# An expert layer's weights one block further ahead, written from another queue and spread in fewer, longer runs

## What is computed

```
def _moe(tokens, router_w, w1, b1, w2, b2):
    logits = tokens.astype(jnp.float32) @ router_w.astype(jnp.float32).T
    probs = jax.nn.softmax(logits, axis=-1)
    rw, re = jax.lax.top_k(probs, TOP_K)
    rw = rw / jnp.maximum(rw.sum(-1, keepdims=True), 1e-12)
    combine = jnp.zeros((N, E), tokens.dtype).at[jnp.arange(N)[:, None], re].set(rw)
    for e in range(E):
        h = jax.nn.gelu(tokens @ w1[e] + b1[e], approximate=False)
        y = h @ w2[e] + b2[e]
        out = out + combine[:, e:e + 1] * y
```

## Time and profile before

| | |
|---|---|
| median of 3 runs | 337.88 us (335.43 to 340.08) |
| the profiled execution | 335.06 us, of which the span of its engines is 333.2 us |
| mean granted clock of TensorE | 0.931 of full speed |
| PE busy | 287.0 us (86%) |
| DVE busy | 220.3 us (66%) |
| ACT busy | 153.3 us (46%) |
| POOL busy | 130.9 us (39%) |
| DMA, all queues | 23.53 MB, mean 71 GB/s |

### The profile page before, as it was taken

One profiled execution on the slowest core, in us unless ns is written; L12 is line 12 of the kernel. 1 busy time (PEld: TensorE's weight loads), 2 busy tenths in 40 slices (PEclk: granted clock), 3 DMA queues, 4 the chain that ended last, 5 costly groups with the idle time before them and its releaser, 6 DMA issues.

```text
span 333.2 us, 9456 instructions
## 1 busy us (share of the span) xinstructions
PE 287.0 (86%) x3821; PEld 184.6 (55%) x3821; DVE 220.3 (66%) x690; ACT 153.3 (46%) x290; POOL 130.9 (39%) x147
## 2 busy tenths in 40 slices
PE   0358799897989888988968999998989999999994
PEld 0348678786656655765645655664434444444551
DVE  5974456775688769667678599756244555557773
ACT  1693621004475465455643445468884454542000
POOL 7326505825995861500013189986008300000000
PEclk9996995555899999999999999999999999999999
DMA  6234000003797596687570000000000001000111
GB/s 229 69 69 94 5 2 2 0 3 85 177 228 165 135 240 165 154 208 188 143 181 2 2 2 1 2 3 3 0 0 2 20 16 33 31 27 8 34 48 48
DMA packets 16903, 23.53 MB, mean 71 GB/s; under 512 B 8052, under 2 KB 12700, under 8 KB 16860
## 3 DMA queue, kind: packets, MB, share of 16 engines
q1 hardware_dynamic: 16860, 22.94, 27.0%
HBM read 20.57 MB, written 2.36 MB: 69 GB/s over the span
## 4 chain that ended last, share of the span: by engine, by line
PE 53%; DVE 14%; DMA 12%; ACT 6%; issue 6%; POOL 5%; SPq 3%; DVEq 0%; POOLq 0%; ACTq 0%
PE pair L1756 8%; PE pair L1741 8%; DMA hid<-c_dram 7%; PE pair L1722 7%; PE pair L1612 5%; PE pair L1390 3%; DMA c_dram<-cT 3%; POOL ln_rstd L585 3%; DVE scaled L840 2%; PE pair L1400 2%; PE pair L1536 2%; PE pair L1563 2%; PE pair L1768 1%; DVE stats L739 1%; DMA xs_ffn<-c_dram 1%
## 5 line engine op out<-in xcount | busy, mean ns | idle before, releaser
L1101 DVE SCALAR_TENSOR_TENSOR hid<-pair,neg_shift,ln_x 128x512 f32<-128x512 f32 x64 | 45.1, 746 | 30.3 <-PE pair L1741 30.3
L1227 ACT ACTIVATE pair<-pair,cols 128x512 f32<-128x512 f32 x64 | 39.5, 656 | 31.0 <-PE pair L1536 30.8
L585 POOL TENSOR_TENSOR ln_rstd<-ln_var,neg_half 128x8 f32<-128x8 f32 x16 | 26.4, 1656 | 50.8 <-DVE ln_var L862 50.8
L1536 PE MATMUL pair<-xs,w1f 64*64 64x256 f32 x512 | 36.6, 402 | 4.2 <-DVE scaled L840 4.1
L1722 PE MATMUL pair<-xs_ffn,f1f 64*64 64x512 f32 x256 | 33.7, 599 | 1.6 <-ACT hid L1299 1.0
L1563 PE MATMUL pair<-scaled,w 64*64 64x256 f32 x512 | 35.0, 378 | 0.0
L1756 PE MATMUL pair<-hid,fo 64*64 64x256 f32 x512 | 34.1, 380 | 0.6 <-DVE hid L1101 0.6
L1612 PE MATMUL pair<-xp,vconv 64*64 64x256 f32 x512 | 32.4, 400 | 0.0
L1756 PEld LDWEIGHTS pair<-hid,fo 64*64 64x64 f32 x512 | 18.6, 133 | 19.9 <-issue 10.9
L840 DVE TENSOR_TENSOR scaled<-pair,hid 128x1024 f32<-128x1024 f32 x16 | 19.5, 1221 | 12.9 <-DMA hid<-c_dram 9.9
L1536 PEld LDWEIGHTS pair<-xs,w1f 64*64 64x64 f32 x512 | 18.2, 138 | 13.6 <-DVE scaled L840 6.0
(11 more groups left out here) (225 smaller groups left out, 559.6 us busy)
## 6 DMA issues: line engine op xcount, KB each, us to landing
xs_ffn<-c_dram SPq DMA_DIRECT2D x32, 256.0 KB, 6.0
hid<-c_dram SPq DMA_DIRECT2D x32, 256.0 KB, 5.4
out_dram<-x SPq DMA_DIRECT2D x8, 256.0 KB, 2.1
x<-in_x_dram SPq DMA_DIRECT2D x3, 512.0 KB, 6.2
x<-in_x_dram SPq DMA_DIRECT2D x2, 256.0 KB, 3.0
w1f<-in_L_ffn_w_dram SPq DMA_DIRECT2D x2, 128.0 KB
w<-in_L_ffn_w_dram SPq DMA_DIRECT2D x2, 128.0 KB
f1f<-in_L_ffn_W_dram SPq DMA_DIRECT2D x2, 128.0 KB
```

Of the source, the lines that this page charges most:

```text
L585: g.tensor_tensor(ln_rstd[:, st, b % 2, :], ln_var[:, st, b % 2, :], neg_half[:, 0:T2], ALU.pow).then_inc(ln_rstd_ready[st], 1)
L1101: v.scalar_tensor_tensor(out=hid2[:, n % 2, u, :].rearrange("p (j n) -> p j n", j=2), in0=h, scalar=neg_shift2[:, k, u:u + 1], in1=w, op0= ...
L1227: s.activation(h, h, ACT.Gelu, bias=cols[:, e:e + 1]).then_inc(hidden_gelu, 1)
L1536: last = t.matmul(pair[N % 2][halves(th), i, 2 * P * u:2 * P * (u + 1)], w1f[halves(i), C * e:C * (e + 1)], xs[halves(i), b % 3, 2 * P * t ...
```

## The change

- The spread is four transfers of 512 KB in 8 KB runs for a block in place of eight of 256 KB in 4 KB runs; the scales of groups 0 and 1 wait for the first two of them, those of groups 2 and 3 for the others.
- The write of cT to DRAM is issued by ACT, right behind its copy, in two halves of 32 rows; SP only waits until both have landed. cw and cT are widened to two halves of 64, the second half of each zero, and the transpose to 128 x 128, so that the halves start at partitions 0 and 64; the bias matmuls thereby work on pieces of 64 rows.
- In round b, DVE routes block b + 2 to the end (before: block b + 2 up to step 14, and the two last steps of block b + 1): steps 1 to 9 behind the scale of group 1, steps 10 to 14 ahead of that of group 3, and 15 and 16 behind it. PE and ACT follow in the order below.
- The scaled tile has three buffers in place of two.
- A gelu on a small tile is put ahead in the start-up, where it loads ACT's table.
- In the start-up the transposes of weights for blocks 0 and 1 stand further ahead, and the two first groups of block 0 in another place among the matmuls of the gates.

```diff
-        b2m = sb("b2m", [T2 * E, T2, C])
+        b2m = sb("b2m", [P, T, C])
...
-        scaled = sb("scaled", [P, 2, 2, 2, 2 * P])
+        scaled = sb("scaled", [P, 3, 2, 2, 2 * P])
...
-        cw = sb("cw", [P, T2 * E])
-        cT = sb("cT", [T2 * E, 2, P])
+        cw = sb("cw", [P, 2, C])
+        cT = sb("cT", [P, 2, P])
...
             for b in range(NB):
-                sp.wait_ge(c_copied, b + 1)
-                sp.dma_start(c_dram.ap()[b].rearrange("h e (r n) -> (h e r) n", r=T), cT[:, b % 2, :]).then_inc(c_written, 16)
-                sp.wait_ge(c_written, 16 * (b + 1))
-                for k in range(KP):
-                    wait(sp, hidden_scaled, KP * (b - 2) + k + 1)
+                sp.wait_ge(c_written[b % 2], 32 * (b // 2 + 1))
+                for k in range(KP // 2):
+                    wait(sp, hidden_scaled, KP * (b - 2) + 2 * k + 2)
                     wait(sp, c_spread[k], 32 * b)
                     for th in range(2):
-                        sp.dma_start(spread[b % 2][halves(th), 2 * k:2 * k + 2, :, :].rearrange("p e i n -> p (e i n)"),
-                                     rep(c_dram.ap()[b, th, 2 * k:2 * k + 2].rearrange("(a e) n -> a (e n)", a=1), 0, C)).then_inc(c_spread[k], 16)
+                        sp.dma_start(spread[b % 2][halves(th), 4 * k:4 * k + 4, :, :].rearrange("p e i n -> p (e i n)"),
+                                     rep(c_dram.ap()[b, th, 4 * k:4 * k + 4].rearrange("(a e) n -> a (e n)", a=1), 0, C)).then_inc(c_spread[k], 16)
...
+            v.memset(cw[:, :, :], 0.0).then_inc(own_zero, 1)
...
+                    op = TT(weights, diff.rearrange("p (h q) -> p h q", h=2), both[:, :].rearrange("p (h q) -> p h q", h=2), ALU.add)
+                op.then_inc(route_step, 1)
...
             def moe_scale(b, k):
                 N = KP * b + k
-                dve.wait_ge(c_spread[k], 32 * (b + 1))
+                dve.wait_ge(c_spread[k // 2], 32 * (b + 1))
                 dve.wait_ge(hidden_gelu, 2 * N + 2)
-                wait(dve, second_done, N - 1)
-                v.tensor_tensor(scaled[:, N % 2].rearrange("p u i n -> p i u n"),
+                wait(dve, second_done, N - 2)
+                v.tensor_tensor(scaled[:, N % 3].rearrange("p u i n -> p i u n"),
                                 pair[N % 2][:, :, :].rearrange("p i (u n) -> p i u n", u=2),
...
                 moe_scale(b, 2)
+                steps(10, 10)
                 if b:
                     moe_add(b - 1)
-                if b + 2 < NB:
-                    route(b + 2, 0, b + 4)
+                steps(11, 11)
+                moe_stat(b + 4, 6)
+                steps(12, 12)
+                moe_stat(b + 4, 7)
+                steps(13, 14)
                 moe_scale(b, 3)
-                if b + 2 < NB:
-                    route(b + 2, 1, b + 4)
+                steps(15, 16)
...
+            s.activation(fm[:, 3, :], neg_half[:, 0:T], ACT.Gelu).then_inc(gelu_table, 1)
...
             def c_copy(b):
                 act_e.wait_ge(c_T, b + 1)
-                wait(act_e, c_written, 16 * (b - 1))
+                wait(act_e, c_written[b % 2], 32 * (b // 2))
                 wait(act_e, second_done, KP * (b - 2) + 1)
-                s.activation(cT[:, b % 2, :], bank[7][0:T2 * E, P:2 * P], ACT.Copy, scale=0.5).then_inc(c_copied, 1)
+                s.activation(cT[:, b % 2, :], bank[7][:, P:2 * P], ACT.Copy, scale=0.5).then_inc(c_copied, 1)
+                act_e.wait_ge(c_copied, b + 1)
+                for th in range(2):
+                    act_e.dma_start(c_dram.ap()[b, th].rearrange("e (r n) -> (e r) n", r=T),
+                                    cT[C * th:C * th + T * E, b % 2, :]).then_inc(c_written[b % 2], 16)
...
             evac_x(1)
             tanh(0)
             c_copy(0)
-            gelu(0, 0)
             gate_relu(2)
             gate_relu(3)
             gate_tanh(2)
             gate_tanh(3)
+            gelu(0, 0)
             gate_out(2)
             gate_out(3)
+            tanh(1)
+            evac_x(2)
...
             def moe_c(b):
-                pe.wait_ge(route_step, 16 * (b + 1))
-                t.transpose(bank[7][0:T2 * E, P:2 * P], cw[:, :], ident[:, :]).then_inc(c_T, 1)
+                pe.wait_ge(route_step, ROUTE * (b + 1))
+                t.transpose(bank[7][:, P:2 * P], cw[:, :, :].rearrange("p h q -> p (h q)"), ident[:, :]).then_inc(c_T, 1)
...
-                for th in (1, 0):
-                    for u in range(2):
+                for u in range(2):
+                    for th in range(2):
                         for i in range(2):
-                            last = t.matmul(pair[2][halves(i), th, P * u:P * (u + 1)], b2m[:, 4 * th + 2 * i + u, :], cT[:, b % 2, :],
-                                            start=(u == 0), stop=False)
-                    if th:
-                        last.then_inc(bias_in, 1)
+                            t.matmul(pair[2][halves(i), th, P * u:P * (u + 1)], b2m[halves(th), 2 * i + u, :], cT[halves(th), b % 2, :],
+                                     start=(u == 0), stop=False)
...
+            moe_c(0)
             third(2)
             third(3)
+            fourth(2)
+            fourth(3)
+            moe_logits(1)
+            gate_conv1(2)
+            gate_conv1(3)
             pe.wait_ge(w_moe, W_MOE)
             pe.wait_ge(conv2_tanh, 2)
             moe_first(0, 0)
-            fourth(2)
-            fourth(3)
-            moe_c(0)
-            moe_logits(1)
-            gate_conv1(2)
-            gate_conv1(3)
             gate_conv2(2)
             gate_conv2(3)
+            pe.wait_ge(conv2_tanh, 4)
+            moe_first(0, 1)
             gate_spread(2)
             gate_spread(3)
-            pe.wait_ge(conv2_tanh, 4)
-            moe_first(0, 1)
+            moe_c(1)
+            moe_x(2)
```

185 lines of the change are left out of this document (98 added, 87 removed).

## The result

The changed kernel takes 346.6 us (median of four runs, 344.4 to 348.1) against 337.8 before: a ratio of 1.030, with a 95% interval of 1.024 to 1.036. It is slower; the forecast was 334.4, with a range up to 341.

A forecast was written before the change was run, and what follows sets the result against it. Spread and write in series were taken to bound the loop at 12.00 us a block; +1.9 + 0.1 + 1.4 - 6.9 = -3.5 on the median of 337.88 gave 334.4 us, range 328 to 341.

The forecast's parts named there:

- What bounds the kernel: Expert loop: the write stands behind the previous spread and the next spread behind the write, 12.00 us a block; TensorE has slack.
- The engines' period: Expert loop: once the DMA hole closes, the engines set the pace, about 11.1 us a block.
- two strings of rows: Expert loop: two chains of engine work, 10.4 and 11.7 us, joined crosswise; two blocks take 22.1.
- PE's string: Expert loop: TensorE's work from the transpose of weights to the end of the next block's first group, 10.4 us.
- the other one: Expert loop: ACT's then DVE's work from first group 0 to the step the next transpose waits for, 11.7 us.
- The cover of the spread: Expert loop: the spread's first 1 MB is ready 9.2 us after the copy begins, against 11.1: 1.9 to spare.
- the six periods: Expert loop, blocks 1 to 7: six intervals take 65.1 us in place of 72.0, a gain of 6.9.
- rival B: Expert loop: the write lands behind the previous spread wherever issued; no change, period 12.0, 339.4 us; chance 0.15.
- The 8 KB runs: Spread transfers: in the loop 0, any faster data ending inside the cover; at block 1 +1.4 us.
- The last block: From the last block on: both kernels do the same work, 0, at best -1 us.
- The start-up: Before the loop: one more first group ahead of the gate spread, +1.9 us, and +0.1 for the second issue.
- the 1.4 of block 1's first scale: Block 1: its first scale waits for 1 MB in place of 0.5 MB, 6.6 us behind the issue, +1.4.

The follow-up runs named there:

- e5: The changed kernel with every spread reading block 0's weights, so SP waits for the first write only; 328.4 and 329.4 us, two further runs 334.8 and 336.7.
- e3: The changed kernel with its spread back in eight transfers of 4 KB runs, each group's scale waiting for its own two; 334.3 us, ratio 0.989.
- e2: The kernel before with only the write of the weights moved to ACT, behind its copy, as one transfer of 64 rows; ratio 1.005.
- e11: The changed kernel with eight transfers of 4 KB runs, its scales still waiting as with 8 KB runs; ratio 1.005.
- e12: The changed kernel with eight transfers of 256 KB in 8 KB runs, each to 32 partitions in place of 64; ratio 1.014.
- e4: The changed kernel with the two halves of the write issued by SP again; 344.1 us, ratio 1.021.
- e13: The changed kernel with eight transfers of 4 KB runs, coarse waits in all blocks but the last, fine waits there; ratio 0.989.
- e10: The changed kernel with 4 KB runs, write from ACT, SP holding back the last group's transfers until ACT's copy, from block 1 on; ratio 0.975.
- e1: The kernel before with only its spread changed, to four transfers of 8 KB runs; ratio 1.019.

## Why the prediction was wrong, step by step

**What bounds the kernel: right.** Spread and write in series set the 12.00, and the engines had slack. e5 shows it: without the round trip the same order runs at 11.15.

**The engines' period: right.** 11.1 was forecast from two strings of rows, 11.15 measured once DMA was out of the way. That the match is so close is in part luck: counted as in the forecast, with the wait of 1.03 at the transpose, PE's string is 11.15 - 1.03 = 10.1 in e5 where 10.4 was forecast, and the other one 11.15 + 1.03 = 12.2 where it was 11.7; the two errors nearly cancel. PE's row of the changed kernel:

```profile
133.50 0.14 PEld L1549 LDWEIGHTS pair<-ident,cw 128*128 128x128 f32 x1 [1.03 <-DVE cw L821]
...
136.51 0.97 PEld L1544 LDWEIGHTS pair<-router,xs 128*128 128x128 f32 x8 [0.39 <-issue]
138.22 0.64 PEld L1561 LDWEIGHTS pair<-xs,w1f 64*64 64x64 f32 x16 [0.74 <-DVE scaled L845]
138.92 0.59 PEld L1572 LDWEIGHTS pair<-cT,b2m 64*64 64x64 f32 x16
139.46 0.69 PEld L1584 LDWEIGHTS pair<-scaled,w 64*64 64x64 f32 x16
```

The bias group takes 0.54 (138.92 to 139.46), below the 0.64 that the forecast took for its floor; the gap ahead of the logits is there, 0.39; the wait at the transpose is 1.03, forecast 0.7. First group 2 waits 0.74 for the scale of group 0, which comes late from DMA; that wait is not in the forecast's strings.

**The cover of the spread: the step that failed.** The forecast said that the spread is issued 2.6 us behind the copy, "1.81 in an idle queue", because the write no longer stands behind the spread. In the changed kernel it is 8.9 (134.14 to 143.03), and the page's row for the write says so too:

```profile
c_dram<-cT ACTq DMA_DIRECT2D x16, 16.0 KB, 6.9
```

6.9 us to land, in the median. The price was taken from an idle queue, although the write is issued in the middle of a spread's data: 5.8 us of them were still to come (134.45 to 140.25). The forecast had counted on about 2 us left, and put these at nothing; the 1.81 behind 2 us would have used up the cover by its own figures. The cover of 1.9 us, on which the whole gain was said to hang, doesn't exist, and the six periods that were to give 6.9 us give none: e3, with everything of the change but the 8 KB runs, runs at 12.26. This is rival B's mechanism, to which 0.15 had been given, and its mark in the traces (a spread late behind its write, scales released by DMA) was named; its 4 to 5 us became 6.9 to 8.6. The Trainium skill, "DMA: Bandwidth & Descriptors", section "Issuing engines are not separate DMA queues", had said that another engine's transfers run on the same 16 DMA engines, and that only the sequencer's time is saved; e2, with 4.5 against 4.2 us, agrees with it read strictly.

**The 8 KB runs: priced at 0 in the loop, measured 1.0 us a block.** The forecast bounded them by a gain only. The longer runs take 9.5 us at 221 GB/s in place of 9.30 at 231, and the hole behind them grows; e11, e12 and the changed kernel put half a microsecond a block on the run length and as much on the four larger transfers. B's period of 12.0 was therefore too short as well: 13.20, which with the last block, below, is why the time lies above B's 339.4. No bound for a loss was given, though no row excluded one; that is why the range ended at 341.

**The last block: "both kernels do the same work: 0".** Wrong by 4.8 us. The coarser wait has nothing to hide behind once no block follows: the first scale of block 7 comes 6.91 behind its spread (168.60 to 175.51) in place of 5.04 (163.03 to 168.07), as this row of the kernel before shows:

```profile
168.07 1.22 DVE L840 TENSOR_TENSOR scaled<-pair,hid 128x1024 f32<-128x1024 f32 x1 [3.78 <-DMA hid<-c_dram]
```

That is 1.9 of the 4.8. Two stretches of the changed kernel at this place, columns as above:

```profile
164.00:175.00 11.00, 8.64 (x148) 5.36 (x148) 5.59 (x7) 6.02 (x10) 0.00 (x0) 1.00 0.73 165
175.00:182.00 7.00, 5.21 (x52) 3.35 (x52) 6.07 (x7) 1.78 (x3) 1.65 (x1) 0.52 0.57 122
```

From 175 to 182 us the granted clock is 0.52; ahead of that PE had stood still, waiting for the last spread, from 172.9 to 176.7, the clock falling at 175.3. Before, it stood still for 3.0 us (166.3 to 169.3), and the clock stayed full behind it:

```profile
164.00:175.00 11.00, 7.51 (x124) 4.74 (x116) 6.41 (x9) 6.00 (x11) 1.65 (x1) 1.00 0.77 192
175.00:182.00 7.00, 5.60 (x72) 3.49 (x76) 6.29 (x11) 2.56 (x7) 2.43 (x2) 1.00 0.01 2
```

The coarser wait alone does not account for the fall. e2, with the fine waits and the old order, has it too, in the slice from 168 to 177 us of its page:

```profile
PEclk9996997655799999999969999999999999999999
```

There PE had stood still for 2.8 us (167.6 to 170.4), less than the 3.0 of the kernel before, which kept the clock. From e2's last spread to its end it takes 172.3 us (164.31 to 336.6) in place of 170.2, while its first scale of block 7 comes no later (4.81 behind the spread), so an estimate for the half clock alone is 2 us, and some 3 for the changed kernel, what the wait leaves of its 4.8. Why the clock falls in one trace and not in another stays open.

**The start-up: wrong sign, small.** +2.0 was forecast for the spread of block 1, -1.6 came. PE's loads in the start-up of the changed kernel:

```profile
75.03 1.78 PEld L1544 LDWEIGHTS pair<-router,xs 128*128 128x128 f32 x8
76.85 0.40 PEld L1451 LDWEIGHTS pair<-yv,gw 64*64 64x64 f32 x6
...
81.85 1.32 PEld L1465 LDWEIGHTS pair<-gspread,same_img 128*128 128x128 f32 x4 [0.76 <-issue]
84.78 0.14 PEld L1549 LDWEIGHTS pair<-ident,cw 128*128 128x128 f32 x1 [1.61 <-DVE cw L821]
```

The gate spread begins at 81.85, where it was 81.98. The step that failed: "the two first groups now both stand ahead of the gate spread". The first of them already did so before, ahead of the fourth matmuls; with it moved, the logits and the first gate convolution come that much earlier, and only one group is new in the stretch, which the waits absorb. The transpose for block 1, at 84.78, is then earlier than the 86.38 of before, not later. The size of the gain is uncertain: in kernels with this start-up order the spread of block 1 is issued at 87.59 (e3), 88.51 (e4), 89.27 (e13), 89.40 (the changed kernel), 89.56 (e12) and 91.38 (e11), in e10's trace, of a run of 338.0 us, even at 94.94; with the old order at 90.57 (e1) to 91.28 (e2). At block 1 itself the first scale comes 8.40 behind the spread's issue (89.40 to 97.80) in place of 5.22, more than the 6.6 forecast; but with the loop bound by DMA that delays no later spread.

On the spans of the two profiles: of the -3.5 forecast, the loop's gain of 6.9 didn't come, the six periods cost 7.2 instead, and the end 4.8; the 1.4 of block 1's first scale delays no spread, and the start-up gave 3.6 more than forecast. -3.5 + 6.9 + 7.2 + 4.8 - 1.4 - 3.6 = +10.4.

## What to carry to other kernels

A small transfer on which the next large one depends has to be priced by the load at the moment at which it is issued, not by an idle queue; a second issuing engine did not move it ahead here. What did help was to hold back the last quarter of the large transfer until the small one was out (0.981 of before in the old kernel, 0.975 in the new order). Fewer and larger transfers also make the first use of the data wait for more of them, and in the new order this showed at the end of the loop, where no other work hides it.
